# Two input loads move from SyncE's DMA queue to ScalarE's, in an attention and feed-forward layer on one core

## The chip, the cores and the metric

The kernel runs on one core of a Trainium2 chip. The time is device microseconds of that core, the median of the runs shown.

## The reference, cut to what matters

Four sequences of 512 rows of 512 pass through attention with 16 query heads of 32 and one shared key and value head, then a layer norm, then a feed-forward part with ternary weights, then a second layer norm.

```python
q = _rotary((x @ Wq + bq).reshape(B, T, H, HD).transpose(0, 2, 1, 3), HD)
k = _rotary((x @ Wk + bk)[:, None], HD)
v = (x @ Wv + bv)[:, None]
scores = jnp.einsum('bhqd,bhkd->bhqk', q, k) / sqrt(HD)
attn = jax.nn.softmax(scores, axis=-1)
ctx = jnp.einsum('bhqk,bhkd->bhqd', attn, v)
x = _layernorm(x + ctx.transpose(0, 2, 1, 3).reshape(B, T, D) @ Wo + bo)
hidden = jax.nn.sigmoid(x @ quantize(w1).T) * (x @ quantize(w2).T)
x = _layernorm(x + hidden @ quantize(w3).T)
```

## The kernel before

Every engine has its own program, and semaphores tie them together. Sequence 0 goes through `first_heads`, with the weights being loaded and rounded beside it. Sequences 1 to 3 go through `heads(b)`: 32 steps k, two for each of the 16 heads, each for 256 query rows. In the same steps the rest of the previous sequence (`s = b - 1`) is done: the output projection, the first norm, and the feed-forward part ("up" and "down").

One step runs through the engines as a pipeline:

- TensorE: two score matmuls (`s_ps`, L1355), and then what the table `BESIDE` puts beside the step. From step 13 on that is mostly "up" (L1310), which needs the bank `a_ps` that ScalarE's `tanh` (L723) drains.
- VectorE: the row maximum (`row_max`, L1046) and, one step later, the low half of p (`p_low`, L1053).
- ScalarE: two exponentials (`exps`, L752), the high half of p (`p_high`, L760), and what its own list puts beside the step: query copies to `raw` (`unit`, L673), normed rows (`h_rows`, L705) and others.
- SyncE (SP): the turning of p by a DMA transpose (`turn`, L477) from `p_all` to `pt_sb`, as soon as VectorE's `p_low` is done.
- GpSimd (POOL): rotations, the stacking of q by DMA (L432), small steps of the norm, and `add_bias` (L573) on x.

The slots of p are four. So the exponentials of a step wait, in `exps`, for the turning of four steps earlier to have landed:

```python
act.wait_ge(maxed, (b * H + h) * TT + (t // 2 + 1) * 2)
if i >= PSLOTS:
    act.wait_ge(turned[n], i // PSLOTS * 16)
```

Two loads go through SP's queue between the turnings. `load_xT(b + 1)` (L459, two DMAs of 512 KB) brings the turned x of the next sequence. It waits until the last query projection (`q3`) of this one is filled, since it overwrites `xT_sb`. `load_x(b)` (L463, one DMA of 1 MB) brings x of this sequence to `xb` for the residual. It waits for ScalarE's `h_rows` of the previous one. TensorE reads the turned x from step 10 on, and GpSimd's `add_bias` reads x.

Of the kernel before, what the change touches and what calls it, by code (L numbers as in the profile page):

```python
# [30 lines left out]
P = 128  # L31
B, T, D, H, F = 4, 512, 512, 16, 1408
HD = D // H
DT = D // P
TT = T // P
# [171 lines left out]
def layer(nc, xT, x, wq, small, wo, b_rows, w1, w2, w3, table, out):  # L207
    with ExitStack() as ctx:
# [11 lines left out]
        q3 = sb("q3", [P, FT * D], I8)  # L220
        b_sb = sb("b_sb", [P, HD + D])
        table_sb = sb("table_sb", [P, 2 * T + 2 * P])
        xT_sb = sb("xT_sb", [P, DT, T])
# [87 lines left out]
        xT_in = [sem(f"xT_in{n}") for n in range(2)]  # L311
# [55 lines left out]
        def filled(use, s, n=0):  # L367

            name = banks_of(use, s)[n]
            return wide[name][1], at(name, use, s)  # L370
# [82 lines left out]
        def _(sp):  # L453
            def load_xT(s):
                if s:
                    sp.wait_ge(*filled("q3", s - 1))
                for half in range(2):
                    cols = slice(half * DT * T // 2, (half + 1) * DT * T // 2)
                    sp.dma_start(xT_sb[:, :, :].rearrange("p k t -> p (k t)")[:, cols],  # L459
                                 xT[s, :, cols]).then_inc(xT_in[half], 16)  # L460

            def load_x(s):
                sp.dma_start(xb, x[s, :, :].rearrange("(t p) d -> p t d", p=P)).then_inc(x_in, 16)  # L463
# [36 lines left out]
                sp.sem_inc(h_free[t], 16)  # L500
            for b in range(1, B):
                for k in range(H * PAIRS):
                    if k == 7 and b < B - 1:
                        load_xT(b + 1)
                    if k:
                        turn(b, *divmod(k - 1, PAIRS))
                    elif b > 1:
                        turn(b - 1, H - 1, 1)
                    if b > 1 and k in (1, 2, 3, 5):
                        store(b - 2, (1, 2, 3, 5).index(k))  # L510
                    if k == 12:
                        sp.wait_ge(h_ready, b * TT)
                        load_x(b)
            turn(B - 1, H - 1, 1)
            for t in range(TT):
                store(B - 2, t)
# [134 lines left out]
        def _(act):  # L651
# [5 lines left out]
            act.dma_start(small_sb[:, :], small).then_inc(small_in, 16)  # L657
            act.dma_start(table_sb[:, :], table).then_inc(table_in, 16)
            act.dma_start(b_sb[:, :], b_rows.partition_broadcast(P)).then_inc(b_in, 16)

            def unit(s, name):

# [147 lines left out]
            def heads(b):  # L810
                s = b - 1
                for k in range(H * PAIRS):
# [25 lines left out]
                        unit(b, "q2")  # L838
                    if k == 6:
                        unit(b, "q3")  # L840
                    if k in (6, 7, 9, 10):
                        h_rows(s, (6, 7, 9, 10).index(k))
                    if k == 10:
# [791 lines left out]
```

## Time and profile before

| | |
|---|---|
| median of 3 runs | 600.63 us |
| the runs | 598.98 to 602.34 us |
| the profiled execution, its own time | 601.29 us |
| its span | 599.4 us |
| mean granted TensorE clock | 0.972 |
| DMA transposes issued by SP | 96 |

The profiled execution is 1.9 us longer than its span, and 0.66 us above the median. A row of the timeline below begins with its start in us, from the start of the span, and its length in us; in brackets stands how long the engine was idle before it, and what ended that.

### The profile page before, as it was taken

The page shows a single profiled execution, that of the slowest core. Times are in us where ns is not written, and L with a number is a line of the kernel's source. Part 1 is how long each engine was busy: PE and PEld are TensorE (multiplying, and loading weights), DVE is VectorE, ACT ScalarE, POOL GpSimd, SP SyncE. Part 2 cuts the span into 40 slices and gives each one's busy share as a digit, 9 for nine tenths or more (in the row PEclk, how much of TensorE's full clock was granted, in tenths as well). Part 3 has the DMA queues.
Part 4 walks back from the last instruction along what each step waited for, and adds up shares of the span by engine and source line. Part 5 has one row for each costly group of instructions (what it writes and reads, how often), then busy time and mean ns, then how long its engine had stood idle before and what let it go on. Part 6 is the DMA issues. An engine that isn't in the chain of part 4 may idle for free.

```text
span 599.4 us, 9184 instructions
## 1 busy us (share of the span) xinstructions
PE 546.4 (91%) x2984; PEld 274.5 (46%) x2984; DVE 476.7 (80%) x639; ACT 420.6 (70%) x857; POOL 299.7 (50%) x398
## 2 busy tenths in 40 slices
PE   9788889898788999999799999999699999989993
PEld 5454445544444444454444445355244444444441
DVE  3788978978998999889989899889989897445433
ACT  2657757779787988787898888678979896233300
POOL 2209796928897734868357335896553300211011
PEclk9779999999979999999999999999799999999997
DMA  8680418239989997999999988989999989000001
GB/s 311 187 310 10 132 41 293 71 65 181 212 147 210 167 181 145 176 193 203 214 199 192 187 163 154 181 187 184 175 217 177 170 177 190 37 0 37 1 0 70
DMA packets 217119, 92.12 MB, mean 154 GB/s; under 512 B 204400, under 2 KB 205552, under 8 KB 216560
## 3 DMA queue, kind: packets, MB, share of 16 engines
q1 hardware_dynamic: 209952, 77.61, 63.9%
q0 software_dynamic: 6144, 12.60, 10.2%
q10 hardware_dynamic: 976, 1.33, 0.6%
q8 instruction: 24, 0.39, 0.3%
q14 instruction: 23, 0.19, 0.1%
HBM read 20.20 MB, written 4.19 MB: 41 GB/s over the span
## 4 chain that ended last, share of the span: by engine, by line
PE 62%; DVE 13%; issue 8%; ACT 8%; DMA 5%; POOL 2%; SPq 1%; ACTq 0%; POOLq 0%; DVEq 0%
PE a_ps L1310 12%; PE b_ps L1310 7%; PE c_ps L1413 7%; PE s_ps L1323 6%; PE s_ps L1355 5%; PE e_ps L1310 5%; DVE p_all L1053 3%; PE b_ps L1323 3%; PE a_ps L1241 3%; DMA pt_sb<-p_all 3%; PE c_ps L1395 3%; ACT p_all L752 2%; PE a_ps L1323 2%; DVE sh_sb L1046 2%; PE s_ps L1366 2%
## 5 line engine op out<-in xcount | busy, mean ns | idle before, releaser
L752 ACT ACTIVATE p_all<-s_ps,sh_sb 128x512 f32<-128x512 f32 x192 | 129.9, 682 | 58.5 <-DVE sh_sb L1046 55.5
L1053 DVE SCALAR_TENSOR_TENSOR p_all<-p_all 128x1024 f16<-128x1024 f32 x96 | 128.6, 1340 | 4.6 <-ACT p_all L760 4.5
L1046 DVE TENSOR_REDUCE sh_sb<-s_ps 128x2 f32<-128x1024 f32 x96 | 116.6, 1215 | 17.2 <-PE s_ps L1355 17.2
L760 ACT ACTIVATE p_all<-p_all 128x1024 f16<-128x1024 f32 x96 | 101.7, 1059 | 2.0
L1310 PE MATMUL a_ps<-late,q 128*128 128x512 f16 x352 | 83.5, 380 | 4.6 <-ACT th L723 2.9
L1355 PE MATMUL s_ps<-k_st,q_st 128*128 128x512 f32 x192 | 79.5, 496 | 2.8 <-ACT p_all L752 1.6
L432 POOL DMA_DIRECT2D q_st<-hi x96 | 49.4, 517 | 59.3 <-PE s_ps L1355 31.4
L561 POOL TENSOR_SCALAR rstd<-mv 128x1 f32<-128x1 f32 x32 | 9.9, 308 | 132.9 <-DVE mv L1013 132.8
L1310 PEld LDWEIGHTS a_ps<-late,q 128*128 128x128 fp8e4 x352 | 31.9, 98 | 47.1 <-issue 7.5
L739 ACT ACTIVATE p_all<-s_ps,sh_sb 128x512 f32<-128x512 f32 x48 | 32.9, 689 | 27.9 <-DVE sh_sb L1040 27.8
L432 POOL DMA_DIRECT2D q_st<-lo x96 | 47.2, 497 | 7.0 <-DVE lo L956 6.7
L1413 PE MATMUL c_ps<-pt_sb,vh 128*32 128x512 f16 x768 | 46.9, 400 | 0.6 <-DMA pt_sb<-p_all 0.5
L1355 PEld LDWEIGHTS s_ps<-k_st,q_st 128*128 128x128 f32 x192 | 34.5, 193 | 26.7 <-issue 15.8
L532 POOL TENSOR_TENSOR rot<-raw,table_sb 128x512 f32<-128x512 f32 x20 | 26.3, 1317 | 39.1 <-ACT raw L673 33.2
L1310 PE MATMUL b_ps<-late,q 128*128 128x512 f16 x192 | 45.4, 379 | 0.0
L537 POOL TENSOR_TENSOR rot<-rot,table_sb 128x512 f32<-128x512 f32 x18 | 23.9, 1328 | 30.8 <-DVE rot L925 30.5
L1310 PE MATMUL e_ps<-late,q 128*128 128x512 f16 x160 | 37.8, 379 | 0.0
L752 ACT ACTIVATION_READ_ACCUMULATOR p_all<-s_ps,sh_sb 128x1 f32 x192 | 37.8, 197 | 0.0
L1241 PE MATMUL a_ps<-xT_sb,wq_sb 128*128 128x512 f32 x72 | 35.6, 611 | 0.8 <-ACT rT L784 0.7
L1040 DVE TENSOR_REDUCE sh_sb<-s_ps 128x1 f32<-128x512 f32 x48 | 31.3, 680 | 3.9 <-PE s_ps L1338 3.8
L1323 PE MATMUL s_ps<-q,late 128*128 128x512 fp8e4 x154 | 34.1, 379 | 0.0
L1413 PEld LDWEIGHTS c_ps<-pt_sb,vh 128*32 128x32 f16 x768 | 20.5, 101 | 24.5 <-issue 8.0
(160 smaller groups left out, 1012.0 us busy)
## 6 DMA issues: line engine op xcount, KB each, us to landing
q_st<-hi POOLq DMA_DIRECT2D x96, 64.0 KB, 3.5
q_st<-lo POOLq DMA_DIRECT2D x96, 64.0 KB, 4.3
late<-in_w SPq DMA_DIRECT2D x2, 2816.0 KB, 14.1
xT_sb<-in_xT SPq DMA_DIRECT2D x8, 512.0 KB, 5.4
late<-in_x SPq DMA_DIRECT2D x4, 1024.0 KB, 6.5
out<-late SPq DMA_DIRECT2D x12, 256.0 KB, 2.9
late<-in_w SPq DMA_DIRECT2D x2, 1408.0 KB, 7.1
q_st<-hi SPq DMA_DIRECT2D x32, 64.0 KB, 2.0
```

Source lines behind the costliest of these rows:

```text
L432: engine.dma_start(q_st[HD * r:HD * (r + 1), slot, :].bitcast(F32), half[HD * (h % HPG):HD * (h % HPG + 1), :].bitcast(F32)).then_inc(stac ...
L739: act.activation(p_sb[:, h % 2, t, :], first_bank(n), ACT.Exp, bias=sh_sb[:, n % (2 * PSLOTS):n % (2 * PSLOTS) + 1], scale=-1.0, accum_out ...
L752: act.activation(p_pair[n][:, t % 2, :], pair_banks(h * PAIRS + t // 2)[:, t % 2, :], ACT.Exp, bias=sh_sb[:, 2 * n + t % 2:2 * n + t % 2 + ...
L760: act.activation(p_half[n][:, 0, :], p_pair[n].rearrange("p t k -> p (t k)"), ACT.Copy, scale=P_SCALE).then_inc(p_hi, 1)
L1040: dve.tensor_reduce(sh_sb[:, n % (2 * PSLOTS):n % (2 * PSLOTS) + 1], first_bank(n), AX.X, ALU.min).then_inc(maxed, 1)
L1046: dve.tensor_reduce(sh_sb[:, 2 * n:2 * n + 2], pair_banks(h * PAIRS + i), AX.X, ALU.min).then_inc(maxed, 2)
L1053: dve.scalar_tensor_tensor(out=p_half[n][:, 1, :], in0=p_pair[n].rearrange("p t k -> p (t k)"), scalar=P_SCALE, in1=p_half[n][:, 0, :], op ...
L1241: mm = pe.matmul(ps[:, :], wq_sb[:, k, g * P:(g + 1) * P], xT_sb[:, k, :], start=(k == 0), stop=(k == DT - 1))
L1310: mm = pe.matmul(ps[:, :], w[:, k, f * P:(f + 1) * P], hT[:, n, k, :], start=(k == 0 and n == 0), stop=(k == DT - 1 and n == 1))
L1323: mm = pe.matmul(ps[:, :], gT[:, n, f, t * P:(t + 1) * P], q3v[:, f, :], start=(f == 0 and n == 0), stop=(f == FT - 1 and n == 1))
L1355: pe.matmul(pair_banks(n)[:, t % 2, :], q_st[:, slot, t * P:(t + 1) * P], k_st[:, b % 2, :], start=True, stop=True).then_inc(scored, 1)
L1413: mm = pe.matmul(c_ps[HD * j:HD * (j + 1), :], vh[:, m, k, :], pt_half[:, (b * H + g * HPG + j) % PTR, :, n, :, k, :], start=(k == 0 and n ...
```

## The change

SP no longer issues the two loads. ScalarE does: the turned x at step 6, behind its copy of the last query group (`unit(b, "q3")`), and x at step 12, behind `p_high`. Each load keeps its wait. The first loads (`load_xT(0)`, `load_xT(1)`, `load_x(0)`) stay in SP's queue.

```diff
             for b in range(1, B):
                 for k in range(H * PAIRS):
-                    if k == 7 and b < B - 1:
-                        load_xT(b + 1)
                     if k:
                         turn(b, *divmod(k - 1, PAIRS))
...
-                    if k == 12:
-                        sp.wait_ge(h_ready, b * TT)
-                        load_x(b)
...
+            def load_xT(s):
+                act.wait_ge(*filled("q3", s - 1))
+                for half in range(2):
+                    cols = slice(half * DT * T // 2, (half + 1) * DT * T // 2)
+                    act.dma_start(xT_sb[:, :, :].rearrange("p k t -> p (k t)")[:, cols],
+                                  xT[s, :, cols]).then_inc(xT_in[half], 16)
+
+            def load_x(s):
+                act.wait_ge(h_ready, s * TT)
+                act.dma_start(xb, x[s, :, :].rearrange("(t p) d -> p t d", p=P)).then_inc(x_in, 16)
...
                     if k == 6:
                         unit(b, "q3")
+                        if b < B - 1:
+                            load_xT(b + 1)
+                    if k == 12:
+                        load_x(b)
```

On ScalarE, around step 6 of sequence 2, this stood before (L752 the exponentials, L760 `p_high`, L673 the copy of q3, L705 `h_rows`):

```order
L752 ACTIVATE p_all,sums<-s_ps,sh_sb 128x512 x2
L760 ACTIVATE p_all<-p_all 128x1024
L673 ACTIVATE raw<-e_ps,small_sb 128x512
L705 ACTIVATE late<-late,shift,rstd 128x512
L752 ACTIVATE p_all,sums<-s_ps,sh_sb 128x512 x2
L760 ACTIVATE p_all<-p_all 128x1024
```

and this stands there now (every line number is six higher):

```order
L758 ACTIVATE p_all,sums<-s_ps,sh_sb 128x512 x2
L766 ACTIVATE p_all<-p_all 128x1024
L679 ACTIVATE raw<-e_ps,small_sb 128x512
L660 DMA xT_sb<-in_xT 128x1024 x2
L711 ACTIVATE late<-late,shift,rstd 128x512
L758 ACTIVATE p_all,sums<-s_ps,sh_sb 128x512 x2
L766 ACTIVATE p_all<-p_all 128x1024
```

Two DMA issues have come between the copy of q3 and the normed rows, ahead of the exponentials of step 7.

On ScalarE, in steps 12 and 13 of sequence 2, this stands now (L729 is `tanh`, L790 copies the row of reciprocals):

```order
L758 ACTIVATE p_all,sums<-s_ps,sh_sb 128x512 x2
L766 ACTIVATE p_all<-p_all 128x1024
L665 DMA late<-in_x 128x4x512
L758 ACTIVATE p_all,sums<-s_ps,sh_sb 128x512 x2
L729 ACTIVATE th<-a_ps 128x512
```

The load of x is the one row that was not there before; it stands ahead of the exponentials of step 13.

On SP, from the load of w3 to the first store, the difference is this (L477 a turning, L470 a store):

```order
-L477 DMA_TRANSPOSE pt_sb<-p_all 128x16x128 x6
-L459 DMA xT_sb<-in_xT 128x1024 x2
-L477 DMA_TRANSPOSE pt_sb<-p_all 128x16x128 x6
-L463 DMA late<-in_x 128x4x512
-L477 DMA_TRANSPOSE pt_sb<-p_all 128x16x128 x21
+L477 DMA_TRANSPOSE pt_sb<-p_all 128x16x128 x33
```

The loads are gone, and the turnings follow each other directly. Sequence 2 differs in the same way, and sequence 3 in its load of x alone.

## Rows read from the trace of the kernel before

**Rows 1.** The page: busy time of the engines, share of the span.

```profile
PE 546.4 (91%) x2984; PEld 274.5 (46%) x2984; DVE 476.7 (80%) x639; ACT 420.6 (70%) x857; POOL 299.7 (50%) x398
```

**Rows 2.** Who waited for whom, ScalarE, 120 to 500 us: total, times, longest.

```profile
ACT p_all L752 <- DVE sh_sb L1046: 55.1, 62, 4.1
ACT p_all L752 <- DMA pt_sb<-p_all: 2.6, 1, 2.6
```

**Rows 3.** The chain that ended last, sequence 1: start, us, what.

```profile
178.86 12.23 DMA pt_sb<-p_all
```

**Rows 4.** All turnings: issue on SP's queue in ns, and us to landing (min/median/max).

```profile
L477 SPq DMA_TRANSPOSE pt_sb<-p_all x96: 1317/2483/6419, 127.3 to 505.6; - x96
...
DMA to landing us min/median/max: 4.2/5.0/12.2
```

**Rows 5.** The three loads of x (L463) after 120 us: time to landing.

```profile
DMA to landing us min/median/max: 6.1/6.8/7.7
```

**Rows 6.** Timeline of SP's queue, steps 12 and 13 of sequence 1.

```profile
173.60 3.72 SPq L477 DMA_TRANSPOSE pt_sb<-p_all  x1
177.37 0.57 SPq L463 DMA_DIRECT2D late<-in_x  x1
178.86 6.42 SPq L477 DMA_TRANSPOSE pt_sb<-p_all  x1
```

**Rows 7.** Timeline of SP's queue, steps 6 and 12 of sequence 2.

```profile
281.01 3.08 SPq L477 DMA_TRANSPOSE pt_sb<-p_all  x1
284.14 1.05 SPq L459 DMA_DIRECT2D xT_sb<-in_xT  x2
...
303.58 5.36 SPq L477 DMA_TRANSPOSE pt_sb<-p_all  x1
308.99 0.57 SPq L463 DMA_DIRECT2D late<-in_x  x1
```

**Rows 8.** Timeline of ScalarE, sequence 1: steps 8, 12, 13 and 16.

```profile
155.90 0.69 ACT L752 ACTIVATE p_all<-s_ps,sh_sb 128x512 f32<-128x512 f32 x1 [2.16 <-DVE sh_sb L1046]
...
173.96 1.06 ACT L760 ACTIVATE p_all<-p_all 128x1024 f16<-128x1024 f32 x1
176.69 0.69 ACT L752 ACTIVATE p_all<-s_ps,sh_sb 128x512 f32<-128x512 f32 x1 [1.68 <-DVE sh_sb L1046]
...
191.18 0.69 ACT L752 ACTIVATE p_all<-s_ps,sh_sb 128x512 f32<-128x512 f32 x1 [2.64 <-DMA pt_sb<-p_all]
```

**Rows 9.** Timeline of TensorE: contexts of sequences 1 and 2, and "up" after step 16.

```profile
169.11 5.56 PE L1413 MATMUL c_ps<-pt_sb,vh 128*32 128x512 f16 x64
...
193.17 1.90 PE L1310 MATMUL a_ps<-late,q 128*128 128x512 f16 x8 [1.68 <-ACT th L723]
...
299.36 3.64 PE L1413 MATMUL c_ps<-pt_sb,vh 128*32 128x512 f16 x64
```

**Rows 10.** Timeline of ScalarE, sequence 2: q3's copy in step 6, steps 7 and 9.

```profile
282.32 0.67 ACT L673 ACTIVATE raw<-e_ps,small_sb 128x512 f32<-128x512 f32 x1
...
285.16 1.06 ACT L760 ACTIVATE p_all<-p_all 128x1024 f16<-128x1024 f32 x1
...
290.83 0.69 ACT L752 ACTIVATE p_all<-s_ps,sh_sb 128x512 f32<-128x512 f32 x1 [1.26 <-DVE sh_sb L1046]
```

**Rows 11.** Timeline of VectorE, sequence 2: the low half of step 7.

```profile
286.91 1.22 DVE L1053 SCALAR_TENSOR_TENSOR p_all<-p_all 128x1024 f16<-128x1024 f32 x1
```

**Rows 12.** Timeline of ScalarE, sequence 2: steps 12, 13 and 14.

```profile
304.63 1.06 ACT L760 ACTIVATE p_all<-p_all 128x1024 f16<-128x1024 f32 x1
305.92 0.69 ACT L752 ACTIVATE p_all<-s_ps,sh_sb 128x512 f32<-128x512 f32 x1 [0.23 <-DVE sh_sb L1046]
...
310.40 0.69 ACT L752 ACTIVATE p_all<-s_ps,sh_sb 128x512 f32<-128x512 f32 x1 [0.53 <-DVE sh_sb L1046]
```

**Rows 13.** Turnings under way at 299 to 300 us (steps 9 and 10, sequence 2).

```profile
L477 SPq DMA_TRANSPOSE pt_sb<-p_all x2: 2273/2380/2486, 296.9 to 299.5; - x2
...
DMA to landing us min/median/max: 6.6/8.0/9.4
```

## The prediction

> **What bounds the kernel now.** I read the page first. TensorE is busy 91% of the span, VectorE 80% and ScalarE 70% [rows 1]. No engine has much room, but the share alone does not say which wait ends last. The waits of ScalarE in the stretch of sequences 1 to 3 come next. Nearly all of its idle time before the exponentials is waiting for VectorE's row maximum, 55.1 us in 62 waits. It waited for a turning of p once only, for 2.6 us [rows 2]. So the turnings, and the loads that stand between them in SP's queue, cost time at one place that the trace shows.
>
> That place is in the chain that ended last. The turning of step 12 of sequence 1 is a link of 12.23 us there [rows 3], while the median turning lands in 5.0 us [rows 4]. The timeline of SP's queue says what stood ahead of it. The load of x was issued at 177.37, the turning at 178.86, and the issue alone took 6.42 us [rows 6] where the median is 2.48 us [rows 4]. The load is 1 MB, and such loads take 6.1 to 7.7 us to land [rows 5]. The turning landed at 178.86 + 12.23 = 191.09, and ScalarE's exponentials of step 16, which need that slot, started at 191.18 after 2.64 us of idleness [rows 8]. TensorE stood still for 1.68 us before it could go on with "up" at 193.17 [rows 9]. So 2.64 us on ScalarE became 1.68 us on TensorE, and 2.64 - 1.68 = 0.96 us of a ScalarE delay is taken up by TensorE's work in hand. I use this 0.96 again below for steps 12 and later.
>
> **What the change removes.** Seven DMA issues go from SP to ScalarE, four for the turned x (two in sequence 1, two in sequence 2) and three for x. SP itself loses 1.05 us for each pair and 0.57 us for each x [rows 7]. SP waits for VectorE's `p_low` most of the time, so this saves nothing by itself. What counts is when the bytes move, and behind what.
>
> *Sequence 1, step 12.* ScalarE ends `p_high` at 173.96 + 1.06 = 175.02 [rows 8] and issues x there. Before, SP did so at 177.37, behind the issue of the turning of step 11 [rows 6]. The load starts 177.37 - 175.02 = 2.35 us earlier, and the turning of step 12 no longer has it ahead in its own queue. If the turning lands 2.35 us earlier, ScalarE's wait falls from 2.64 to 0.29 us, and TensorE's stop of 1.68 us is gone, since 2.35 is more than 1.68. Bounds of this term: 0 (the same bytes go over the same DMA engines, and the turning lands as late as before) and -1.68 us (TensorE's whole stop). I take -1.68, since the move is by more than it needs.
>
> **What it adds.** *The issues on ScalarE.* The trace has no issue of ScalarE beside a turning. From SP's rows a pair for the turned x takes 1.05 us and x takes 0.57 us [rows 7]. The nearest lower value is the same work with nothing in the way; the upper is a ScalarE held until SP's turning is issued, a rival below.
>
> - Step 6, sequence 1: the pair stands ahead of steps 7 and 8. ScalarE then was idle for 2.16 us before the exponentials of step 8, waiting for the row maximum [rows 8]. 1.05 us fits into it: 0.
> - Step 6, sequence 2: ScalarE has no idle time up to step 9, where it has 1.26 us [rows 10]. What is behind the issues is `p_high` of step 7, which ended at 285.16 + 1.06 = 286.22 [rows 10]. VectorE, which is the busy engine in this stretch, took it up at 286.91 [rows 11]. The spare time is 0.69 us; 1.05 - 0.69 = +0.36 us.
> - Step 12, sequence 1: 0.57 us fits into the 1.68 us of idleness before step 13 [rows 8]: 0. Sequence 3 is taken to be the same.
> - Step 12, sequence 2: the idleness before step 13 is 0.23 us [rows 12]. 0.57 - 0.23 = 0.34 us on ScalarE, less than the 0.96 us that TensorE takes up: 0.
>
> *The load of x beside turnings under way, sequence 2.* ScalarE is through with `p_high` at 304.63 + 1.06 = 305.69 [rows 12], where SP issued x at 308.99 [rows 7]: 3.3 us earlier. But at 305.69 the turning of step 10 is still in flight. It was issued at 299.5 and took 9.4 us, so it landed at 308.9 [rows 13]. Step 14's exponentials, which need it, started at 310.40 [rows 12]: 1.5 us to spare. Its last 308.9 - 305.69 = 3.2 us now share the DMA engines with the load. At worst they take twice as long, 3.2 us more, which is 3.2 - 1.5 = 1.7 us late on ScalarE and 1.7 - 0.96 = 0.74 us on TensorE. At best nothing, as its packets are ahead. I take +0.3, near the middle.
>
> **The sum.** -1.68 + 0.36 + 0.3 = -1.02 us. The profiled execution took 601.29 us, so it would take 600.3. The median of the runs is 0.66 us lower, so I forecast 600.63 - 1.0 = **599.6 us**. A measurement of this kernel tells about 0.5% from no change, that is 3.0 us; its own runs lie 3.4 us apart. The forecast is inside that.
>
> **The rivals.**
>
> *The bytes decide, not the queue.* The load and the turnings share the same DMA engines. If the turning of step 12 lands as late as before, the gain of 1.68 us is gone and the costs stay: +0.36 + 0.3 = +0.7 us, 601.3 us. For it: the load needs 6 to 8 us wherever it is issued [rows 5]. Against it: it starts 2.35 us earlier. The Trainium skill has a rule for this, in "DMA: Bandwidth & Descriptors", section "Issuing engines are not separate DMA queues": starting DMAs from several engines saves only the time to start them. By that rule the time would be this rival's.
>
> *ScalarE is held by SP's turnings.* This one ends on the other side. A turning is not issued in a moment: SP's queue is taken for 1.3 to 6.4 us [rows 4], and longer where transfers are piled up. If what makes SP wait also holds an issue of ScalarE, then ScalarE stands until SP's turning is issued, with the whole softmax behind it. Step 6 of sequence 2: ScalarE is ready at 282.32 + 0.67 = 282.99 [rows 10], SP is done at 281.01 + 3.08 = 284.09 [rows 7]. 1.10 + 1.05 - 0.69 = +1.46 us. Step 12 of sequence 2: ready at 305.69, SP done at 303.58 + 5.36 = 308.94. 3.25 + 0.57 - 0.23 = 3.59 us on ScalarE, less 0.96 = +2.63 us. Step 12 of sequence 1: ready at 175.02, SP done at 173.60 + 3.72 = 177.32 [rows 6]. 2.30 + 0.57 - 1.68 - 0.96 = +0.23 us, and as much in sequence 3. The load then starts no earlier, so the gain is 0. Sum +4.6 us: 605.2 us. It decides the sign once ScalarE is held in sequence 2's step 12 by more than 0.96 + 0.23 + 1.0 us or so. For it: SP's issues stretch to 5.36 and 6.42 us in just the stretches where ScalarE must issue. Against it: no row shows two queues issuing together beside a turning, and SP's own load went out in 0.57 us right behind the 5.36 us of a turning. The same page of the Trainium skill, section "Queues, rings and completion order", says that SP and ScalarE each have a ring on every DMA engine but no descriptor generator of their own. No run shown so far bears on it, and it speaks for this rival, not for the forecast.
>
> *TensorE's clock.* The context of head group 0 took 5.56 us in sequence 1 and 3.64 us in sequence 2 for the same 64 matmuls [rows 9], the first in a stretch at half clock (1.2 GHz). If the shifts of a microsecond here end such a stretch, 5.56 - 3.64 = 1.9 us come back at the least: 597.7 us. If they bring one to sequence 2, it is 601.5 us.
>
> **How the numbers follow.** Forecast 38%. Bytes decide: 16%. ScalarE held: 28%. A half-clock stretch fewer 14%, one more 4%. Slower by over 0.5% (above 603.6) is the held ScalarE alone: 28%. Faster by over 0.5% (below 597.6) would need the clock and the whole gain: I give it the 14%. The rest, 58%, is within 0.5%. The likeliest case's own range is 598.5 to 601.0. The range for 8 in 10 reaches from the clock's case to the held ScalarE's sum: 597.2 to 605.4 us.
>
> **What would show it.** Right: ScalarE's issue rows at steps 6 and 12 last 0.4 to 0.6 us each; the turning of step 12 in sequence 1 lands within about 10 us; ScalarE no longer waits for `pt_sb` there, and TensorE's 1.68 us before "up" are gone. For the second rival: issue rows on ScalarE of 1.5 us and more, ending with SP's turning. For the first: the same 2.6 us wait for `pt_sb`. Wrong altogether would be a new wait of ScalarE for a turning in steps 14 to 17 of sequences 2 or 3, longer than the one removed.

## The result, and the profile after

| | before | after |
|---|---|---|
| median | 599.81 us, 4 runs | 615.92 us, 4 runs |
| the runs | 598.98 to 602.34 us | 608.6 to 617.69 us |
| the profiled execution | 601.29 us | 615.58 us |
| its span | 599.4 us | 613.7 us |
| mean granted TensorE clock | 0.972 | 0.959 |

The change makes the kernel slower by 2.3%: the ratio is 1.0231, with a 95% interval of 1.0186 to 1.0275. That it is slower is clear; whether by more than 2% isn't. The forecast was 599.6 us, with 605.4 as the upper end of the range. It missed on both sign and size.

From the page of after: the engines' busy time (against [rows 1]), and the three loads of x with KB each and us to landing.

```profile
PE 553.4 (90%) x2984; PEld 276.6 (45%) x2984; DVE 477.7 (78%) x639; ACT 420.4 (69%) x857; POOL 295.5 (48%) x398
...
late<-in_x ACTq DMA_DIRECT2D x3, 1024.0 KB, 12.1
```

ScalarE, VectorE and GpSimd do what they did. TensorE is busy for 7.0 us more than in [rows 1], with the same 2984 matmuls. The span is 14.3 us longer, so TensorE is also idle for 14.3 - 7.0 = 7.3 us more. The loss has two halves, then: stops, and matmuls that take longer. The loads of x land in 12.1 us where they took 6.8 [rows 5].

The two lines that were moved, in after: issue time on ScalarE's queue in ns (min/median/max), then us to landing.

```profile
L660 ACTq DMA_DIRECT2D xT_sb<-in_xT x4: 335/526/1152, 149.6 to 287.9; - x4
...
DMA to landing us min/median/max: 5.0/7.0/11.1
```

```profile
L665 ACTq DMA_DIRECT2D late<-in_x x3: 385/385/402, 175.1 to 442.2; - x3
...
DMA to landing us min/median/max: 8.9/12.1/15.9
```

So the issues themselves are cheap, 0.34 to 1.15 us. ScalarE isn't held. What went wrong is in the second line of each fence, and in the turnings. All 96 turnings of after, with the same columns (against [rows 4]):

```profile
L477 SPq DMA_TRANSPOSE pt_sb<-p_all x96: 1654/2528/10536, 126.9 to 519.9; - x96
...
DMA to landing us min/median/max: 4.3/5.1/16.8
```

The median turning is as before, 5.1 against 5.0 us. The longest went from 12.2 to 16.8 us. Who waited for whom on ScalarE in sequences 1 to 3 of after (against [rows 2]: total, times, longest):

```profile
ACT p_all L758 <- DVE sh_sb L1056: 53.6, 57, 4.1
ACT p_all L758 <- DMA pt_sb<-p_all: 16.0, 4, 5.1
```

Before, ScalarE waited once for a turning, 2.6 us. Now it waits four times, 16.0 us. The timeline of ScalarE in after says where (start, us; the idle time before it in brackets). Sequence 1, load of x at step 12, then the exponentials of steps 15 and 16:

```profile
175.13 0.40 ACTq L665 DMA_DIRECT2D late<-in_x  x1
...
190.50 0.69 ACT L758 ACTIVATE p_all<-s_ps,sh_sb 128x512 f32<-128x512 f32 x1 [4.68 <-DMA pt_sb<-p_all]
...
195.22 0.69 ACT L758 ACTIVATE p_all<-s_ps,sh_sb 128x512 f32<-128x512 f32 x1 [1.35 <-DMA pt_sb<-p_all]
```

Sequence 2, the turned x at step 6 and the exponentials of step 9; sequence 3, x at step 12 and the exponentials of step 15:

```profile
287.44 1.08 ACTq L660 DMA_DIRECT2D xT_sb<-in_xT  x2
...
300.41 0.69 ACT L758 ACTIVATE p_all<-s_ps,sh_sb 128x512 f32<-128x512 f32 x1 [4.88 <-DMA pt_sb<-p_all]
```

```profile
442.22 0.39 ACTq L665 DMA_DIRECT2D late<-in_x  x1
...
458.10 0.69 ACT L758 ACTIVATE p_all<-s_ps,sh_sb 128x512 f32<-128x512 f32 x1 [5.13 <-DMA pt_sb<-p_all]
```

The slot that step 15 waits for was read by the turning of step 11. That is one step earlier than the turning of step 12, the only one that was late before. The chain that ended last names the same one in sequence 1, as its longest link (start, us, what; against [rows 3]):

```profile
174.76 15.65 DMA pt_sb<-p_all
```

It had been issued 0.37 us before the load, and in before it landed in 5.5 us. Issue and landing of all of them around the load of x in sequence 1, read from the two traces:

```
                        before                      after
turning of step 11      173.60 -> 179.08  (5.5)     174.76 -> 190.42 (15.7)
load of x               177.37            SP        175.13 -> 187.25 (12.1)  ScalarE
turning of step 12      178.86 -> 191.10 (12.2)     180.05 -> 195.14 (15.1)
```

By the prediction the turning of step 12 should have landed 2.35 us earlier. It landed 195.14 - 191.10 = 4.0 us later, of which 1.2 us is the later start of this stretch.

How much the DMA engines moved while this went on: packets, mean rate, and the share of each queue (q1 is SP's, q10 ScalarE's, q0 GpSimd's), 177 to 189 us of after:

```profile
DMA packets 2733, 1.85 MB, mean 155 GB/s; under 512 B 2155, under 2 KB 2155, under 8 KB 2732
...
q1 hardware_dynamic: 2067, 0.52, 59.3%
q10 hardware_dynamic: 528, 1.05, 42.1%
q0 software_dynamic: 137, 0.27, 14.5%
```

The same steps of sequence 1 in before, 179 to 191 us, with the load and the turnings in one queue and GpSimd's copies of q (its stacking, L432) beside them:

```profile
DMA packets 3709, 2.30 MB, mean 192 GB/s; under 512 B 3085, under 2 KB 3085, under 8 KB 3708
...
q1 hardware_dynamic: 3452, 1.76, 97.2%
q0 software_dynamic: 256, 0.52, 16.1%
```

The shares of the packets' time add up to more than the 16 engines' whole time in both, 113% before and 116% after. So packets were under way all the time, and yet 155 GB/s were moved where it had been 192. In sequence 3 it is 130 GB/s (446 to 458 us of after) where before moved 230 (441 to 453 us). Call this the crawl: a turning takes 2.3 to 3.0 times as long as in before, a load of x 1.6 to 2.6 times (12.1 against 7.7 us in sequence 1, 15.9 against 6.1 in sequence 3), and fewer bytes land.

TensorE then pays twice. Its timeline in after, behind ScalarE's wait in sequence 1 (against [rows 9], 1.68 us idle):

```profile
184.64 1.90 PE L1320 MATMUL a_ps<-late,q 128*128 128x512 f16 x8
...
192.49 3.60 PE L1320 MATMUL a_ps<-late,q 128*128 128x512 f16 x8 [3.76 <-ACT th L729]
```

The same eight matmuls of "up" took 1.90 us before the stop of 3.76 us and 3.60 us behind it. The windows of TensorE in after (length, busy us and instructions, granted clock, DMA share, GB/s) show the granted clock around the three stops:

```profile
176.00:188.00 12.00, 12.00 (x59) 1.00 1.19 158
188.00:200.00 12.00, 8.24 (x26) 0.72 1.14 189
...
299.00:311.00 12.00, 7.01 (x32) 0.72 1.19 201
...
458.00:470.00 12.00, 9.91 (x38) 0.86 1.13 205
```

The stops (3.76 us, several of 0.6 to 2.4 us in sequence 2, 4.23 us) are each followed by a fall from full (2.4 GHz) to half clock (1.2 GHz) for a part of the window: 0.72, 0.72 and 0.86. The same steps of before stayed at full clock, in sequences 2 and 3 too (1.00 from 291 to 303 us and from 446 to 456). In sequences 1 and 3:

```profile
187.00:196.00 9.00, 7.32 (x35) 1.00 1.01 204
...
446.00:456.00 10.00, 10.00 (x48) 1.00 1.11 194
```

By the turnings' issue times, after less before, the loss builds up like this: -0.4 us at step 0 of sequence 1, +1.2 from step 5 on (ahead of the first moved load, and found at +0.6 to +1.8 in most of the other profiles below too, so not counted as the change's), +6.1 from step 16 of sequence 1, +8.5 behind step 16 of sequence 2, where +9.6 had been reached at step 11, and +14.3 from step 17 of sequence 3. So x in sequence 1 cost 4.9 us, the turned x in sequence 2 2.4 us, x in sequence 3 5.8 us. The turned x in sequence 1 and x in sequence 2 cost nothing that lasted.

### The profile page after: what moved, and what is told of

It is laid out like the page before. It is cut to its first block, busy times and chain, and to the rows that moved or that the text cites. A ratio compares the mean times of both kernels' runs of the same rounds, so it can differ in the third digit from the quotient of the medians.

```text
span 613.7 us, 9184 instructions
## 1 busy us (share of the span) xinstructions
PE 553.4 (90%) x2984; PEld 276.6 (45%) x2984; DVE 477.7 (78%) x639; ACT 420.4 (69%) x857; POOL 295.5 (48%) x398
## 3 DMA queue, kind: packets, MB, share of 16 engines
q0 software_dynamic: 6144, 12.60, 10.5%
## 4 chain that ended last, share of the span: by engine, by line
PE 61%; DVE 12%; DMA 9%; issue 7%; ACT 6%; POOL 2%; SPq 1%; POOLq 0%; ACTq 0%; DVEq 0%
PE a_ps L1320 11%; DMA pt_sb<-p_all 8%; PE c_ps L1423 6%; PE b_ps L1320 6%; PE s_ps L1333 5%; PE e_ps L1320 5%; PE s_ps L1365 5%; DVE p_all L1063 3%; PE b_ps L1333 3%; PE a_ps L1251 3%; PE c_ps L1405 2%; PE a_ps L1333 2%; DVE sh_sb L1056 2%; PE s_ps L1376 2%; ACT p_all L758 2%
## 5 line engine op out<-in xcount | busy, mean ns | idle before, releaser
L1320 PE MATMUL a_ps<-late,q 128*128 128x512 f16 x352 | 86.0, 389 | 9.7 <-ACT th L729 8.0
L432 POOL DMA_DIRECT2D q_st<-hi x96 | 49.4, 517 | 72.6 <-ACT hi L688 41.2
L432 POOL DMA_DIRECT2D q_st<-lo x96 | 47.2, 497 | 6.9 <-DVE lo L966 6.5
L1365 PEld LDWEIGHTS s_ps<-k_st,q_st 128*128 128x128 f32 x192 | 34.7, 194 | 28.0 <-issue 14.7
L527 POOL TENSOR_TENSOR rot<-raw,table_sb 128x512 f32<-128x512 f32 x20 | 26.4, 1319 | 38.4 <-ACT raw L679 32.5
L1320 PE MATMUL e_ps<-late,q 128*128 128x512 f16 x160 | 39.8, 394 | 0.0
L1012 DVE SCALAR_TENSOR_TENSOR b_ps<-th,b_ps 128x512 f32<-128x512 f32 x24 | 16.7, 695 | 24.4 <-PE b_ps L1320 14.4
L1050 DVE TENSOR_REDUCE sh_sb<-s_ps 128x1 f32<-128x512 f32 x48 | 31.2, 680 | 3.9 <-PE s_ps L1348 3.9
## 6 DMA issues: line engine op xcount, KB each, us to landing
late<-in_x ACTq DMA_DIRECT2D x3, 1024.0 KB, 12.1
```

The costliest lines, as they stand in the source:

```text
L432: engine.dma_start(q_st[HD * r:HD * (r + 1), slot, :].bitcast(F32), half[HD * (h % HPG):HD * (h % HPG + 1), :].bitcast(F32)).then_inc(stac ...
L1050: dve.tensor_reduce(sh_sb[:, n % (2 * PSLOTS):n % (2 * PSLOTS) + 1], first_bank(n), AX.X, ALU.min).then_inc(maxed, 1)
L1320: mm = pe.matmul(ps[:, :], w[:, k, f * P:(f + 1) * P], hT[:, n, k, :], start=(k == 0 and n == 0), stop=(k == DT - 1 and n == 1))
L1365: pe.matmul(pair_banks(n)[:, t % 2, :], q_st[:, slot, t * P:(t + 1) * P], k_st[:, b % 2, :], start=True, stop=True).then_inc(scored, 1)
```

## The experiments

Each version of the kernel ran with the kernel before beside it on the same chip, which had a median of 601.6 to 602.2 us; the ratios are to those runs. Line numbers differ by a few from kernel to kernel. Code is cut to the lines that matter; a line taken away is one of the changed kernel, and in the last version one of the kernel before. The theories set against each other, however the expectations number them: a load and a turning in two queues at once slow each other down (those under number 1; 1b is the one in which GpSimd's copies, as the third, are needed for it); ScalarE, or the work behind its issue, is held; the bytes alone decide; or the place among the steps does, with the queue of no account.

**Each load alone.** Only x goes to ScalarE; the turned x stays in SP's queue.

```diff
+                    if k == 7 and b < B - 1:
+                        load_xT(b + 1)          # SP
...
-                        if b < B - 1:
-                            load_xT(b + 1)      # ScalarE
```

> The kernel before with only the load of x (1 MB, step 12) on ScalarE's queue; the turned x stays in SP's. Theory 1, that a turning in flight and a load from a second queue slow each other down: the loads of x land in 9 to 16 us instead of 6 to 8, the turning of step 11 in sequences 1 and 3 in about 15 us, and 8 to 12 of the change's 14 to 16 us are here, so 607 to 612 us. Theory 2, that the turned x is what costs (its issue stands ahead of step 7, and its load meets the turning of step 5): no more than 2 us over before, 602 us at most.

Measured: 610.86 us (607.4 to 612.38), ratio 1.0133, interval 1.0091 to 1.0175. ScalarE's waits, and its exponentials of step 15 in sequence 3:

```profile
ACT p_all L753 <- DMA pt_sb<-p_all: 11.2, 3, 5.9
```

```profile
454.89 0.69 ACT L753 ACTIVATE p_all<-s_ps,sh_sb 128x512 f32<-128x512 f32 x1 [5.92 <-DMA pt_sb<-p_all]
```

The same crawl at the same steps: the issue takes 0.37 us (at 438.04) and the slot comes 5.92 us late. By the turnings' issue times x costs 2.4 us in sequence 1 and 6.8 us in sequence 3.

The other way round, only the turned x goes to ScalarE, with x back on SP.

```diff
+                    if k == 12:
+                        sp.wait_ge(h_ready, b * TT)
+                        load_x(b)               # SP
...
-                    if k == 12:
-                        load_x(b)               # ScalarE
```

> The kernel before with only the turned x (two loads of 512 KB, step 6, sequences 1 and 2) on ScalarE's queue; x stays in SP's. Theory 1: its loads too meet a turning in flight, that of step 5, which in the changed kernel landed after 7.8 and 13.4 us; half the bytes and two sequences, so 3 to 5 us over before, 603 to 605 us. Theory 2: nearly the whole 14 us. A theory 3, that ScalarE's time for the issues costs and nothing else: 0 to 1 us.

Measured: 603.42 us (600.52 to 609.75, 10 runs), ratio 1.0035, interval 1.0 to 1.0069. The profiled one is among its long ones, 608.79 us, and shows why: in sequence 2 the turning of step 5 took 17.1 us, and ScalarE stood for 8.65 us (the issue of the pair, and the exponentials of the step that waited).

```profile
280.94 1.10 ACTq L663 DMA_DIRECT2D xT_sb<-in_xT  x2
297.68 0.69 ACT L757 ACTIVATE p_all<-s_ps,sh_sb 128x512 f32<-128x512 f32 x1 [8.65 <-DMA pt_sb<-p_all]
```

So each load can crawl by itself, though the median loss of the turned x alone is small, and its interval begins at no loss. With x all four runs are long. With the turned x the ten runs spread over 9.2 us, as if it crawled in some executions only, but one profile doesn't show that.

**Kept apart in time.** Is it the overlap? x is issued by ScalarE at step 13, once the turning of step 11 has landed, and SP issues the next turning only when x has landed.

```diff
+                    if k == 13:                 # SP
+                        sp.wait_ge(x_in, (b + 1) * 16)
...
-                    if k == 12:                 # ScalarE
+                    if k == 13:
+                        act.wait_ge(turned[3], ((b - 1) * H * PAIRS // PSLOTS + 3) * 16)
                         load_x(b)
```

> x on ScalarE's queue, but never beside a turning: ScalarE issues it one step later, behind the high half of step 13, and waits for the turning of step 11 to have landed; SP issues the turning of step 12 only when x has landed. The turned x stays with SP. Theory 1: the load lands in 6 to 8 us again, and the turning of step 12 lands at about the same place as in the kernel before, so 598 to 604 us, however late SP is made to wait. If ScalarE's queue or its issue were slow in itself, the load would take 9 us and more here too, and the time would be that of the run with x alone on ScalarE, or more.

Measured: 606.81 us (605.24 to 608.95), ratio 1.0088, interval 1.0055 to 1.012. Landing of the three loads, and ScalarE's waits:

```profile
DMA to landing us min/median/max: 5.3/5.8/5.8
```

```profile
ACT p_all L755 <- DMA pt_sb<-p_all: 10.7, 5, 3.0
```

Without a turning beside it the load lands in at most 5.8 us, so ScalarE's queue isn't a slow one. But holding the turnings back costs ScalarE nearly as much waiting as the crawl did (10.7 us in five waits, against 11.2), and the kernel took 606.8 us, longer than the 598 to 604 that were expected. Two things were changed at once here, the hold and the step. This run alone doesn't say which of them took the crawl away.

**The place alone.** The same as before this one, with nothing held: ScalarE issues x at step 13.

```diff
-                    if k == 12:                 # ScalarE
+                    if k == 13:
                         load_x(b)
```

> x on ScalarE's queue at step 13, as in the run that kept it apart from the turnings, but with nothing held: the turnings go on. The turned x stays with SP. Theory 1 (what costs is the load beside turnings, wherever it starts): the load takes 9 us and more, turnings beside it 10 us and more, 608 to 613 us, above the 606.8 of the run kept apart. If the place alone (step 12) had been bad: the load lands in 6 to 8 us, and the time is at or below 606.8 us.

Measured: 601.0 us (598.45 to 602.38, 10 runs), ratio 0.998, interval 0.996 to 1.0001. The expectation missed. It is the same queue and the same bytes as the first experiment, one step later, and the 1.3% are gone.

```profile
ACT p_all L753 <- DMA pt_sb<-p_all: 2.1, 2, 1.8
```

In sequence 1 the load goes out at 179.41, 0.56 us *ahead* of the turning of step 12 (179.97), with the turning of step 11 nearly through (landed 180.36, 5.7 us). The load lands in 7.2 us; the turning of step 12 lands in 11.5 us, about as in before, and is needed late enough. Sequence 3 tells more. There the load goes out at 438.78, 0.36 us *behind* the turning of step 12, as close as in the slow run of sequence 1 of after (0.37 us). But GpSimd's copies have all landed by then, and this turning lands in 7.6 us:

```profile
L477 SPq DMA_TRANSPOSE pt_sb<-p_all x1: 1825/1825/1825, 438.4 to 438.4; - x1
...
DMA to landing us min/median/max: 7.6/7.6/7.6
```

So a load in ScalarE's queue costs nothing by being there; what it meets decides. From SP's queue the load couldn't meet it in this way, since SP issues one DMA behind the other ([rows 6]).

**Another queue.** x goes through GpSimd's own queue, behind the rotation of q3, with its own semaphore.

```diff
+                if s:                           # add_bias
+                    pool.wait_ge(x_pool, s * 16)
...
                 rotation(b, "q3")
+                pool.wait_ge(h_ready, b * TT)
+                pool.dma_start(xb, x[b, :, :].rearrange("(t p) d -> p t d", p=P)).then_inc(x_pool, 16)
```

> x in GpSimd's queue, behind the rotation of q3, at about the time at which SP issued it; GpSimd then waits for it in the same place as before. ScalarE issues nothing. Theory 1b (three queues at once): the load and GpSimd's copies are now in one queue, so there are two at most, and the time is within 3 us of before. Theory 1a (any load beside turnings): turnings of steps 11 and 12 take 10 us and more, 606 to 612 us. If it were ScalarE's own issues that cost: within 2 us of before.

Measured: 601.63 us (599.36 to 603.19, 10 runs), ratio 0.9991, interval 0.9969 to 1.0013: no change. ScalarE's waits for a turning, and the landing of the loads:

```profile
ACT p_all L755 <- DMA pt_sb<-p_all: 2.8, 1, 2.8
```

```profile
DMA to landing us min/median/max: 6.7/7.9/9.9
```

In GpSimd's queue the load stands in line with GpSimd's own copies of q, and it begins at 179.66 in sequence 1, again with the turning of step 11 nearly through. Both the theory of three queues and that of ScalarE's own issues had this time, so it doesn't part them; but a load beside turnings alone is not enough to cost time.

**Without GpSimd's copies.** The first experiment again, with the copies of q for heads 8 and up held until x has landed.

```diff
+                pool.wait_ge(x_in, (b + 1) * 16)
                 stack(pool, b, 8)
```

> x alone on ScalarE's queue at step 12, as in the run that was slow, but GpSimd's copies of q for heads 8 and 9 (8 copies of 64 KB each side of it in time) wait until x has landed. So turning 11 and the load are in flight together without copies. Theory 4 (a turning under way and the load, packet by packet, are enough): the load still takes 10 to 17 us and turning 11 14 to 18 us, 608 to 613 us. Theory 1b (the copies put the DMA engines out of step, and only then do both crawl): load 6 to 8 us, turning 11 at most 10 us, about 603 us, what is left being the late copies of q.

Measured: 604.99 us (604.12 to 607.73, 9 runs), ratio 1.0065, interval 1.0042 to 1.0087. Landing of the turnings from 168 to 185 us, and the rate from 172 to 182:

```profile
L477 SPq DMA_TRANSPOSE pt_sb<-p_all x4: 1877/2636/4051, 167.5 to 180.8; - x4
...
DMA to landing us min/median/max: 4.3/6.9/7.5
```

```profile
DMA packets 4761, 2.29 MB, mean 229 GB/s; under 512 B 4204, under 2 KB 4204, under 8 KB 4760
...
q1 hardware_dynamic: 4158, 1.05, 48.9%
```

Load and turning meet as in the first experiment, at step 12, and there is no crawl: 229 GB/s, and the turning that the load joined took 7.5 us here (8.0 in sequences 2 and 3), the loads at most 8.0. A packet of a turning took 48.9% of 16 x 10 us / 4158 = 19 ns; in the crawl of after it was 59.3% of 16 x 12 us / 2067 = 55 ns. ScalarE waits for a turning once, for 0.4 us. The kernel is still 0.65% slower. The waits that are new are for GpSimd's work, which the hold makes late: a rounding of weights (L552), and copies of q that TensorE waits for:

```profile
ACT late L733 <- POOL q L552: 2.9, 1, 2.9
PE s_ps L1359 <- DMA q_st<-lo: 3.4, 2, 2.1
```

TensorE's busy time is 546.5 us, that of before [rows 1]: its longest new stop is 2.1 us, and the clock's mean is 0.973, against 0.972 before.

**The whole change, later.** Everything as in the changed kernel, but the turned x at step 8 and x at step 13.

```diff
-                        if b < B - 1:
-                            load_xT(b + 1)
-                    if k == 12:
+                    if k == 8 and b < B - 1:
+                        load_xT(b + 1)
+                    if k == 13:
                         load_x(b)
```

> The whole change, both loads on ScalarE's queue, but issued later: the turned x at step 8 in place of 6, x at step 13 in place of 12. Theory 5, that the moment decides (the load must not meet a turning whose packets are already going, and the turning behind it must be the one with time to spare): x costs nothing, as in the run at step 13, and the turned x depends on whether a turning is under way at step 8; 600 to 606 us. If the queue itself were at fault: 612 us and more again, as for the change.

Measured: 615.83 us (611.28 to 617.62), ratio 1.0222, interval 1.0172 to 1.0272. The expectation of 600 to 606 us missed. The time is that of the branch in which the queue itself is at fault, but the waits are others than in the change:

```profile
ACT raw L679 <- PE c_ps L1251: 12.8, 2, 8.5
ACT p_all L758 <- DMA pt_sb<-p_all: 2.8, 2, 1.7
```

```profile
309.35 3.78 PE L1251 MATMUL c_ps<-xT_sb,wq_sb 128*128 128x512 f32 x4 [5.83 <-DMA xT_sb<-in_xT]
```

x is as harmless as in the step-13 experiment (landed in 6.2 to 6.5 us). The turned x is not: at step 8 it meets a turning and GpSimd's copies again, its second half lands in 11.3 and 14.4 us beside turnings of 12.3 and 15.4 us, and now TensorE itself waits for it at step 10. It waits four times, 15.9 us in all. A place that is safe for one load isn't one for the other.

**The DMAs by themselves.** Three kernels do nothing but DMAs: they leave out all computation. Each runs stretches of eight turnings with loads of 1 MB beside them, in one queue or another, each stretch ended by a wait for all of it.

> Only DMAs, none of the computation: six stretches one after the other, each ended before the next begins. 8 turnings of 128x2048 fp16 from SP: alone (0), with 3 loads of x between them in SP's queue (1), with the 3 loads on ScalarE's queue beside them (2), the 3 loads alone (3), 8 turnings with 3 loads of turned x, rows of 4096 bytes in place of 2048, on ScalarE's queue (4), 8 turnings with 12 copies of 64 KB from GpSimd's queue (5). If the DMA engines only share their time, stretch 2 lasts as long as stretch 1, and both about stretch 0 plus stretch 3: some 8 x 2.6 = 21 us and 3 x 4.3 = 13 us, 34 us. Theory 1: stretch 2 is longer than stretch 1 by 10 us or more, stretch 4 too, and stretch 5 is longer than its parts.

> Only DMAs again, nine stretches of which eight hold 8 turnings from SP. The load of 1 MB now starts in mid-stream (when two turnings have landed), not at the start of a stretch: turnings alone (0), load in SP's queue (1), load in ScalarE's queue (2); then the same three with 8 copies of 64 KB from GpSimd's queue at the same moment (3, 4, 5); load of turned x with the copies in SP's queue (6) and in ScalarE's (7); load and copies without turnings (8). Theory 1a, that a second queue beside a turning in mid-stream is enough to make both crawl: stretch 2 is over 5 us longer than stretch 1. Theory 1b, that it takes three queues (turnings, load, and GpSimd's copies): 2 is no longer than 1, and 5 is over 5 us longer than 4. If neither, 5 equals 4, and the crawl of the real kernel needs something that is not a DMA.

> Only DMAs, eleven stretches of 8 turnings with one load of 1 MB each. In stretches 0 to 7 a turning is issued when the one before has landed, some 4.4 us apart, about as in the kernel: none (0), load in SP's queue ahead of the fourth turning (1), in ScalarE's at the same moment (2), in ScalarE's 1.2 us later (3); with 12 copies of 64 KB from GpSimd begun one turning earlier: load in SP's (4), in ScalarE's at once (5), 1.2 us (6), 2.4 us (7) later. In 8 to 10 the turnings come without a pause, with 16 copies begun one turning before the load: SP's, ScalarE's at once, ScalarE's 1.8 us later. Theory 1b: 5, 6, 7, 9 or 10 is over 4 us longer than 4 or 8, with the load at 10 us and more; 2 and 3 are as long as 1. Theory 4: 2 or 3 too. If all with ScalarE's load are within 1 us of SP's, the crawl needs the real kernel's other engines or its stores.

Their stretches, in us from the first issue to the last landing, from the traces:

```
first kernel, three loads            second kernel, one load
  8 turnings alone       21.8          8 turnings alone               21.9
  + loads in SP's queue  33.0          + load in SP's queue           25.0
  + loads in ScalarE's   29.2          + load in ScalarE's            24.8
  3 loads alone          10.8          + load, SP's, and copies       28.6
  + turned x, ScalarE's  29.0          + load, ScalarE's, and copies  28.8
  + 12 copies, no load   26.3          + turned x, SP's, copies       29.3
                                       + turned x, ScalarE's, copies  30.7
third kernel, one load, a turning issued only when the one before has landed
  none; SP's queue; ScalarE's at once; ScalarE's 1.2 us later         34.4; 37.7; 37.7; 36.4
  with 12 copies: SP's; ScalarE's at once; 1.2 us; 2.4 us later       40.1; 40.7; 38.4; 38.3
third kernel, turnings without a pause, load about the fourth, 16 copies begun just before
  load in SP's queue                      31.2   (load 10.3, longest turning 12.1)
  load in ScalarE's queue, at once        31.6   (load 11.6, longest turning 14.2)
  load in ScalarE's queue, 1.8 us later   33.8   (load 14.7, longest turning 16.0)
```

The theory that a second queue as such costs throughput fell in the first kernel: three loads from ScalarE's queue took less time (29.2 us) than from SP's (33.0). Nor did a third queue with copies do it when all began together (28.6 against 28.8), and with turnings that wait for each other a load that joined one late in ScalarE's queue was even the faster one (38.4 and 38.3 against 40.1). Theory 1b had asked for over 4 us, and no stretch gave that. The nearest is the last, where the load joins a turning that is under way, with copies pending: 2.6 us longer than with SP's queue, and the load at 14.7 us instead of 10.3. The rate from 382 to 396 us, and the landing of the two turnings around the load there:

```profile
DMA packets 3702, 2.41 MB, mean 172 GB/s; under 512 B 3032, under 2 KB 3032, under 8 KB 3702
```

```profile
L288 SPq DMA_TRANSPOSE pt_sb<-p_all x2: 3594/4466/5337, 375.8 to 379.5; - x2
...
DMA to landing us min/median/max: 8.2/12.1/16.0
```

In SP's stretch, from 318 to 332 us, the rate is 224 GB/s. So a part of the crawl comes up without any computation. The price is small for all bytes together, 33.8 - 31.2 = 2.6 us, and larger for one turning in flight, 16.0 us against 12.1. But 12.1 us is already long, in SP's own queue, by the load's bytes and the copies alone. The queue makes 1.3 times of it, where the real kernel had 2.3 to 3.0. Each stretch ran once.

**A version that beats both.** If order in one queue is good, and the only loss of before was one turning behind 1 MB, then x can be cut: four loads of 256 KB in SP's queue, ahead of the turnings of steps 11 to 14, with a semaphore each.

```diff
-                    if k == 12:
-                        sp.wait_ge(h_ready, b * TT)
-                        load_x(b)
+                    if k in (12, 13, 14, 15):
+                        if k == 12:
+                            sp.wait_ge(h_ready, b * TT)
+                        load_x(b, [k - 12])
...
-                pool.wait_ge(x_in, (s + 1) * 16)
+                pool.wait_ge(x_in[t], (s + 1) * 16)
```

> A try for a version better than both: x stays in SP's queue, but as four loads of 256 KB ahead of the turnings of steps 11 to 14 in place of one of 1 MB at step 12. The turning of step 12 in sequence 1 then has a quarter of the bytes ahead of it, lands in about 8 us instead of 12.2, and ScalarE's wait of 2.64 us and TensorE's of 1.68 us go: 0 to 2 us faster than before, 599 to 602 us. A rival: each load brings its own two to three microseconds of start and landing into the queue, the turnings of steps 12 to 15 are all later by a little, and nothing is gained.

> The load of x of the later sequences stays in SyncE's queue, cut into four loads of 256 KB ahead of the turnings of steps 11 to 14, with a semaphore each; the kernel is the one that gave a ratio of 0.9967 (0.9932 to 1.0002) in three rounds. If the delay that turning 12 takes from the load ahead of it is worth the 1.68 us stop of TensorE in sequence 1 and a like one in sequence 3, the ratio is 0.994 to 0.998 with an interval below 1. If TensorE gives the stop back elsewhere (it is full for 90% of the span, and its clock granted varies), the ratio is 0.999 to 1.001.

Measured: first 600.37 us (596.5 to 605.24, 10 runs), ratio 0.9967, interval 0.9932 to 1.0002; then, on another chip, 598.75 us (596.99 to 600.47, 7 runs), ratio 0.995, interval 0.9925 to 0.9974. Of the two only the second is clear of no change: 0.5% faster than before. The trace is of the second. SP's queue in sequence 1 (against [rows 6]), and ScalarE's waits for a turning (against [rows 2]):

```profile
179.95 3.51 SPq L478 DMA_TRANSPOSE pt_sb<-p_all  x1
```

```profile
ACT p_all L754 <- DMA pt_sb<-p_all: 0.8, 1, 0.8
```

The turning of step 12 lands 8.7 us after its issue instead of 12.2, and the wait of 2.6 us is 0.8. What TensorE waited for behind `tanh` in before (total, times, longest) has no such line left:

```profile
PE a_ps L1310 <- ACT th L723: 2.9, 2, 1.7
```

These are the 1.68 us that the prediction wanted back, in sequence 1, and 1.25 us in sequence 2 (at 329.9, not in sequence 3 as the expectation had it). With x at step 13 on ScalarE's queue the same wait was 1.9 us in three pieces of up to 0.8, and the kernel at 0.998, with no change inside its interval. So they were there to be had, most of all by a shorter piece ahead of the turning; a cut load on ScalarE's queue was not tried.

## Why the prediction was wrong

*What bounds the kernel.* Right. The one wait for a turning was real, and taking most of it away in SP's own queue gave 0.5%, though not all of that is this wait's: 3.0 us between the medians, where 1.68 us had been at stake in sequence 1.

*The issues on ScalarE.* The durations were about right: a pair was put at 1.05 us and took 1.51 and 1.08, x was put at 0.57 and took 0.39. But they cost ScalarE nothing, since they didn't wait for its work in hand, as the prediction had them do. In sequence 2 the pair went out at 287.44, while `p_high` ran (287.33 + 1.06), and ahead of the copy of q3 (288.29); from `p_high` of step 6 to that of step 7 it is 3.79 us in after and 3.80 in before. The +0.36 us for it was 0. For the same reason x went out at 175.13, as `p_high` of step 12 began (175.12), and not at its end, 1.05 us later. It came 0.37 us behind the turning of step 11, where the prediction's own times put it 175.02 - 173.60 = 1.42 us behind. The rival of the held ScalarE gave 605.2 us and had the right sign, which is luck, but its mechanism is refuted: SP's turning at 441.24 took 6.01 us to issue, and ScalarE's load went out in the middle of it, at 442.22, in 0.39 us. The two turnings that SP issued at 437.5 and 441.2 us in after:

```profile
L477 SPq DMA_TRANSPOSE pt_sb<-p_all x2: 3025/4516/6007, 437.5 to 441.2; - x2
```

*The term of -1.68 us. This is the step that failed.* It said that the load starts 2.35 us earlier, "and the turning of step 12 no longer has it ahead in its own queue". It bounded the term by 0 on the bad side, "the turning lands as late as before". It looked at the turning behind the load and not at the one in front. In SP's queue the load was issued only when the issue of the turning of step 11 was done (173.60 + 3.72 = 177.32, then 177.37). From ScalarE's queue, with GpSimd's copies pending, the load joined it, and the turning of step 11 went from 5.5 to 15.7 us. It is needed at step 15, one step before the one that was late. The wait of 4.68 us on ScalarE, less the 0.96 us that TensorE takes up, is 3.72 us; TensorE's stop was 3.76. In sequence 3 it is 5.13 - 0.96 = 4.17 against 4.23. That part of the working, how a ScalarE delay turns into a TensorE stop, held to 0.06 us.

*The load beside a turning, +0.3 us.* The mechanism was named, for sequence 2 alone, and bounded by "at worst they take twice as long". There it did no harm. In sequences 1 and 3 the turning took 2.9 and 2.3 times as long as in before (15.7 against 5.5, 16.8 against 7.4), and at step 6 of sequence 2 3.0 times (13.4 against 4.5). A bound of twice, from sharing the engines evenly at an unchanged rate, is no bound when the rate falls, from 192 to 155 GB/s in sequence 1 and from 230 to 130 in sequence 3. "Sequence 3 is taken to be the same" as sequence 1 did hold, for the loss.

*The turned x, +0.36 us.* Put at the issue time alone, which cost nothing; the load cost 2.4 us in sequence 2, by the same crawl.

*"The bytes decide."* Too small as well, at 601.3 us. By the rule of the Trainium skill that it rested on ("DMA: Bandwidth & Descriptors", "Issuing engines are not separate DMA queues") another engine saves only the time to start. The runs bear it out with x at step 13 (0.998) and in GpSimd's queue (0.9991). They don't at step 12, where the same bytes took the kernel 610.86 us.

*TensorE's clock.* Considered as luck of a microsecond here or there, in both directions. It is a consequence: the three stretches with stops in after each fell to half clock, and TensorE's busy time rose by 7.0 us. A stop should have been priced with what follows it, in sum about twice its length here (7.3 us idle, 7.0 us slower matmuls). The part differs: by the windows, at most 0.28 x 12 = 3.4 us go with the stop of 3.76 us, and at most 0.14 x 12 = 1.7 us with that of 4.23. A slip beside it: the case of a half-clock stretch fewer comes to 597.7 us, not below the 597.6 that its 14% was given to.

*What was listed as "wrong altogether"* was a new wait of ScalarE for a turning in steps 14 to 17 of sequences 2 or 3, longer than the one removed. That is what came, in sequence 3 at step 15 with 5.13 us, and in sequence 1 too. It had no number of its own.

**What stays open.** Why the rate falls isn't settled: the rows read here don't say which of the 16 engines a packet was on. What the profiles of all versions show together is when it comes. A load from ScalarE's queue was issued within 1.5 us behind a turning's issue in 17 places. In seven of them no copy of GpSimd's was pending (the turned x in sequence 1 of after and of the version with the turned x alone, x in sequence 3 twice when issued at step 13, and the three with the copies held), and the turning took 7.5 to 8.0 us. In ten a copy was, and in eight of these the turning took 12.3 to 17.8 us. So the pending copies are needed as far as these profiles go, and they aren't enough: x in sequence 2 met eight pending copies in after and seven when alone, and the turning took 9.8 and 10.5 us. Why the same kernel lies between 608.6 and 617.69 us, and the one with the turned x alone between 600.5 and 609.8, fits a crawl that comes or not by small shifts, but that was only argued; one profile of each was taken.

## What to carry to other kernels

That one engine issues its DMAs one behind the other also protects: before a load is moved to another queue, list what is in flight at its new moment, and who needs *that* first, not only what it stood ahead of. Where one transfer that something waits for sits behind a large load, cut the load and spread it over the same queue before trying another queue. Price a stop of TensorE of some us with the slower clock behind it, here 7.0 us of slower matmuls for 7.3 us of stops.

## What the runs showed of the hardware

- A load of 1 MB from a second queue stretched a DMA transpose already under way from 5.5 to 15.7 us, with the load itself at 12.1 instead of 7.7, while copies of GpSimd's were pending. Packets were under way all the time, and 155 GB/s were moved instead of 192. With GpSimd's copies held it was 229 GB/s and 7.5 us.
- A DMA issue on ScalarE wasn't delayed by SP's transposes: 0.39 us, in the middle of one of SP's that took 6.01 us to issue. Nor does it wait for ScalarE's activation in hand: issued at 175.13, beside one of 1.06 us that began at 175.12.
- Shifting the load by one step (4.5 us) took the loss from 1.3% to nothing measurable.
- Behind stops of 3.76 and 4.23 us, and several shorter ones close together, TensorE's granted clock was at half for a part of the next 12 us (0.72, 0.72, 0.86), where a stop of 1.68 us in before was not followed by it.
